# Paired row statistics, roots on ScalarE, the hidden layer computed ahead, and the dense rows' mean taken off on VectorE

## The chip, the cores and the metric

The kernel is one program on one core of a Trainium2 chip. The metric is the device time in microseconds (us), the median over several executions. All data is fp32, and the whole layer is one launch.

## The reference, cut to what matters

A graph network layer over N = 100,000 nodes with 160 features and 25,000 edges, sorted by their destination. It has two halves, and each begins with a layer norm and a ReLU of the node rows. Only the parts that the change touches are spelled out.

```python
def _layernorm(x, axis=-1, eps=1e-05):
    m = jnp.mean(x, axis=axis, keepdims=True)
    v = jnp.var(x, axis=axis, keepdims=True)
    return (x - m) / jnp.sqrt(v + eps)

h = jnp.maximum(_layernorm(x, axis=-1), 0.0)
x = x + _L0_gnn_ref(h, node_vec1, edge_attr_4, edge_attr_8, ...)   # sc(h), lin1(h)[src], edge net, lin2, cos and sin of an angle
h = jnp.maximum(_layernorm(x, axis=-1), 0.0)
x = x + _L1_gnn_ref(h, edge_attr_4, ...)                           # message of h[src], segment_sum, relu
# inside _L0_gnn_ref, for every edge:
h = jax.nn.silu(edge_scalars @ fc_w1 * (1.0 / np.sqrt(8.0)))
weight = h @ fc_w2 * (1.0 / np.sqrt(64.0))
```

Because the deviation is positive, relu((x - m) / s) is relu(x - m) / s. The kernel uses this in the first half: only the mean is taken off before the matrix products, and 1/s is multiplied in afterwards, together with `node_vec1`.

## The kernel before, in words

The kernel runs in a start and three phases, with five engines that each follow their own written list of steps; semaphores join them. In the tables below a stage ends where the next one's first work begins.

**The start** builds index tables from the sorted edges, stores them to DRAM with SyncE's queue (lines 410 to 419), multiplies weights together and scales them. SyncE waits for the stores (`s_tab_out`) and then loads the first edge quad.

**Phase 1** goes over 98 dense units `u` of 1024 nodes (128 partitions x `GD` = 8 rows; `U` = 98) and at the same time over 196 edge tiles of 128 edges. Four tiles make a quad `q` (`GQ` = 4; `Q` = 49), so a quad goes with two units. For a unit, VectorE takes `bn_stats` of each of the 8 rows (`dense_stats`, line 1334), and three parts of small instructions turn the two half-row moments that `bn_stats` leaves into minus mean and variance (`moment_part`, lines 1203 to 1210; `rest_of`, line 1215, takes the mean off the first 32 columns). ScalarE takes the mean off the other 128 columns with the ReLU in the same instruction (`dense_relu`, line 763, 8 instructions), TensorE transposes the rows (`dense_tr`, line 964), ScalarE copies them from PSUM (`dense_copy`, line 770), TensorE multiplies (`linear`, lines 969 and 970), VectorE adds the result times a scale to x (`dense_x1`, line 1353) and takes the statistics of the new rows (`dense_stats2`, line 1362, and again `moment_part`). GpSimd raises the variance to the power -0.5 (`inverse_root`, line 628), forms the scale and the shift (lines 635 and 642), ScalarE writes the normed rows (`dense_h1`, line 755), and GpSimd adds them to x (`dense_y`, line 625). Two DMAs store both.

For an edge quad GpSimd gathers the source rows (`p1_gather`, line 581, four indirect DMAs), the same statistics, moments, ReLU (line 782) and transposes follow; TensorE's `net_mm` and ScalarE's `net_silu` (lines 1025 and 775) compute the hidden layer of the quad; then each tile goes through `p1_source`, the features on VectorE (lines 1421, 1426, 1430), `p1_feat_t` (line 1083), `p1_parts`, the message (lines 1402, 1409) and `p1_sum` (line 1069). Each engine's order inside a unit is written in its `step(u)`, which has two halves, `slot(u, 0)` and `slot(u, 1)`. TensorE's `dense_tr` waits until ScalarE has copied the sum of `p1_sum` out of the same PSUM bank (`e_tot`, line 810).

**Phase 2** goes over the 49 quads again. GpSimd gathers the destination rows (`p2_gather`, four indirect DMAs at line 581) and later scatters the new h rows (`p2_scatter`, four at line 587). Between them lie on VectorE the statistics (line 1528), moments, eight small angle steps (`p2_angle`, lines 1543 to 1560), scales, the sums at lines 1589 and 1599, the second statistics (line 1608) and moments. Here the root is already ScalarE's (`p2_root1`, `p2_root2`, lines 896 and 901), and each quad switches ScalarE's function table to the sine and back.

**Phase 3** computes the second half's messages over the 196 tiles; the change does not touch it.

Of the kernel before, what the change touches and what calls it, by code (L numbers as in the profile page):

```python
# [19 lines left out]
P = 128  # L20
GD = 8
# [53 lines left out]
def gnn_kernel(nc, xa, src, dst, number, edges_in, scalars_in, scalars_t_in, wpack, out):  # L75
# [19 lines left out]
    sum_tab = scratch("sum_tab", (Q, P, GQ * CW))  # L95
    y_tab = scratch("y_tab", (Q, P, GQ * D))
# [23 lines left out]
    with ExitStack() as ctx:  # L120
# [34 lines left out]
        minus_half = sb("minus_half", [P, GD])  # L155
# [21 lines left out]
        st1, st2 = four("st1", [P, GD, 6]), two("st2", [P, GD, 6])  # L177
        su1, su2 = four("su1", [P, GD, 2]), two("su2", [P, GD, 2])
        df1, df2 = four("df1", [P, GD]), two("df2", [P, GD])
        sq1, sq2 = four("sq1", [P, GD]), two("sq2", [P, GD])  # L180
        m21, m22 = four("m21", [P, GD]), two("m22", [P, GD])
        neg1, neg2 = four("neg1", [P, GD]), two("neg2", [P, GD])
        var1, var2 = four("var1", [P, GD]), two("var2", [P, GD])
# [16 lines left out]
        q_sct = two("q_sct", [GQ * SW, P])  # L200
# [5 lines left out]
        hr_e = two("hr_e", [P, GQ * 32])  # L206
# [9 lines left out]

        x_q = [x_all[:, i * GQ * XW:(i + 1) * GQ * XW] for i in range(4)]
# [4 lines left out]
        st_e = two("st_e", [P, GQ, 6])  # L222
        su_e = two("su_e", [P, GQ, 2])
        df_e = two("df_e", [P, GQ])
        sq_e = two("sq_e", [P, GQ])
        m2_e = two("m2_e", [P, GQ])
        neg_e = two("neg_e", [P, GQ])
        var_e = two("var_e", [P, GQ])
        sd_e = two("sd_e", [P, GQ])
        sd2 = two("sd2", [P, GQ])  # L230
# [38 lines left out]
        n_act = sem("net_hidden_ready")  # L269

        d_in = [sem(f"x_loaded{i}") for i in range(4)]
        d_ln1 = sem("dense_moments1")
        d_relu = sem("dense_h_ready")
# [6 lines left out]
        d_ln2 = sem("dense_moments2")  # L280
        d_h1 = sem("dense_h1_ready")
# [5 lines left out]
        e_tb = sem2("p1_tables_loaded")  # L287
        e_scl = sem("p1_scale_ready")
        e_g = sem2("p1_source_rows")
        e_ln = sem("p1_moments")  # L290
        e_relu = sem("p1_h_ready")
# [27 lines left out]
        r_relu = sem("p2_h_ready")  # L319
# [31 lines left out]
        def x3(t, w, g):  # L351
            return t[:, :].rearrange("p (g f) -> p g f", g=g, f=w)

# [14 lines left out]
        def _(sp):  # L368
# [53 lines left out]
            sp.wait_ge(s_rows, 32)  # L422
            sp.wait_ge(s_tab_out, 16 * n_out)
# [16 lines left out]
            def p1_load(q):  # L440
                j = q.mod(2)
                wait(sp, e_g[j], q.over(2, 64))
                sp.dma_start(i_src[j][:, :], src_tab[q.times(1)]).then_inc(e_ix[j], 16)
                wait(sp, n_mm, q.times(1, -1))
                sp.dma_start(q_sct[j][:, :], scalars_t[q.times(1)]).then_inc(n_in[j], 16)
# [121 lines left out]
        def _(pool):  # L567
            nc.gpsimd.memset(t_next[:, :], N + 5).then_inc(s_fill, 1)
            nc.gpsimd.memset(t_prev[:, :], -1).then_inc(s_fill, 1)
            nc.gpsimd.memset(minus_half[:, :], -0.5)  # L570
# [40 lines left out]
            def p1_gather(q):  # L611
                j = q.mod(2)
                pool.wait_ge(e_ix[j], q.over(2, 16, 16))
                wait(pool, e_relu, q.times(1, -1))
                wait(pool, e_scl, q.times(2, -2))
                gather(xa, x_e[j], XW, i_src[j], e_g[j])
# [10 lines left out]
            def inverse_root(inv, var, n, signal):  # L627
                nc.gpsimd.tensor_tensor(inv[:, 0:n], var[:, 0:n], minus_half[:, 0:n], ALU.pow).then_inc(signal, 1)  # L628

            def dense_scale(u):  # L630
                j = u.mod(4)
                pool.wait_ge(d_ln1, u.times(5, 4))
                inverse_root(inv1[j], var1[j], GD, d_scl)
                pool.wait_ge(d_scl, u.times(2, 1))
                nc.gpsimd.tensor_tensor(scl1[j][:, :], inv1[j][:, :], x3(x_in[j], XW, GD)[:, :, D], ALU.mult).then_inc(d_scl, 1)

            def dense_norm2(u):
                j = u.mod(2)
                pool.wait_ge(d_ln2, u.times(4, 4))
                inverse_root(inv2[j], var2[j], GD, d_nmr)  # L640
                pool.wait_ge(d_nmr, u.times(2, 1))
                nc.gpsimd.tensor_tensor(nmr2[j][:, :], neg2[j][:, :], inv2[j][:, :], ALU.mult).then_inc(d_nmr, 1)  # L642
# [9 lines left out]
            def step(w):  # L652
                q = At(w.i, w.c // 2, 2)
                if w.mod(2) == 1 and (q + 1).within(Q):
                    p1_gather(q + 1)
                if (w - 1).within(U):
                    dense_scale(w - 1)
                if (w - 4).within(U):
                    dense_y(w - 4)
                if (w - 3).within(U):  # L660
                    dense_norm2(w - 3)
                if w.mod(2) == 0 and q.within(Q):
                    p1_scale(q)
# [3 lines left out]
            for w in range(8):  # L667
                step(At(0, w))
            with pool.Fori(2, U // 4) as i:
                for c in range(4):  # L670
                    step(At(i, c))
            for w in range(U - 2, U + 4):
# [74 lines left out]
        def _(act):  # L747
# [11 lines left out]
            def dense_relu(u, h):  # L759
                act.wait_ge(d_ln1, u.times(5, 3))  # L760
                x, hh = x_in[u.mod(4)], hb[u.mod(2)]
# [1080 lines left out]
```

## Time and profile before

| what | value |
|---|---|
| time, median of 3 runs | 2476.07 us (2475.62 to 2479.8) |
| profiled execution, first to last instruction | 2863.6 us |
| instructions | 55863 |
| busy share of the span: PE, PEld, DVE, ACT, POOL | 68%, 64%, 68%, 54%, 61% |
| mean granted TensorE clock | 0.828 of full |
| HBM traffic | 130 GB/s over the span |

The profiled execution's own time is given only as its span, 2863.6 us; nothing around the span is on the page. It is 387.5 us more than the median of the runs. PE is TensorE's matmul, PEld its weight load, DVE is VectorE, ACT is ScalarE, POOL is GpSimd and SPq SyncE's queue. A busy share is an average over the phases.

### The profile page before, as it was taken

The numbers are of one execution on the slowest core, as the hardware profiler recorded it, in microseconds if no ns is written. First come the engines' busy times: TensorE is split into PE (matmuls) and PEld (weight loads), VectorE is DVE, ScalarE is ACT, GpSimd is POOL, SyncE is SP. The second block draws the span as 40 slices with busy tenths as digits, with TensorE's granted clock in tenths as the row PEclk, the third lists the DMA queues.
The fourth block names the chain that finished last, engine by engine and source line by source line (L and its number), as shares of the span: only waits on it lengthen the run. The fifth ranks groups of instructions, "written<-read, shape, count | busy, mean of one in ns | idle before, by whom it ended". The sixth has DMA issues, their size and how long they took to land.

```text
span 2863.6 us, 55863 instructions
## 1 busy us (share of the span) xinstructions
PE 1940.9 (68%) x12874; PEld 1820.7 (64%) x12874; DVE 1954.7 (68%) x8628; ACT 1560.1 (54%) x4412; POOL 1745.2 (61%) x1676
## 2 busy tenths in 40 slices
PE   0888888878878888878883343434344777777877
PEld 0777777777877777777773333323233777767777
DVE  2889888887888888888884655556555444444444
ACT  0667677776777777777774444545453222222222
POOL 1656666665666666766656565655565666666665
PEclk9989999998999999999995555555555999999898
DMA  9444544443444444454543232323332333333332
GB/s 79 142 143 169 172 170 171 172 172 138 169 172 170 173 169 164 162 179 147 180 154 124 87 89 87 93 87 97 88 99 83 81 89 88 92 92 90 94 95 74
DMA packets 223602, 364.52 MB, mean 127 GB/s; under 512 B 115938, under 2 KB 133149, under 8 KB 223405
## 3 DMA queue, kind: packets, MB, share of 16 engines
q1 hardware_dynamic: 176524, 289.81, 32.1%
q0 software_dynamic: 47040, 74.31, 9.8%
q14 instruction: 27, 0.21, 0.0%
q8 instruction: 11, 0.18, 0.0%
HBM read 176.85 MB, written 194.78 MB: 130 GB/s over the span
## 4 chain that ended last, share of the span: by engine, by line
DVE 31%; PE 25%; issue 14%; another core or an unknown queue 11%; POOL 8%; ACT 6%; SPq 2%; DMA 1%; DVEq 1%; ACTq 0%; POOLq 0%
DVE st L1334 3%; PE bank L969 3%; PE bank L1154 3%; POOL x_e L581 3%; POOL inv L628 3%; DVE x L1353 2%; DVE su_e L1203 2%; PE bank L964 2%; PE bank L1166 2%; DVE st L1362 2%; PE bank L1163 2%; ACT h L755 2%; PE bank L1176 2%; DVE x L1599 2%
## 5 line engine op out<-in xcount | busy, mean ns | idle before, releaser
L628 POOL TENSOR_TENSOR inv<-var,minus_half 128x8 f32<-128x8 f32 x196 | 327.7, 1672 | 256.5 <-DVE var L1210 253.4
L625 POOL TENSOR_TENSOR yo<-x,h 128x640 f32<-128x640 f32 x196 | 305.8, 1560 | 147.8 <-ACT h L755 145.4
L969 PE MATMUL bank<-wp,hT 128*128 128x160 f32 x1568 | 392.6, 334 | 1.6 <-DVE x L1353 0.7
L755 ACT ACTIVATE h<-x,nmr,inv 128x160 f32<-128x160 f32 x784 | 342.2, 514 | 6.1 <-POOL nmr L642 6.1
L587 POOL DMA_INDIRECT h_all<-h,i_put x196 | 203.4, 1038 | 217.9 <-ACT h L871 146.0
L964 PE MATMUL bank<-ident,h_e 128*128 128x128 f32 x392 | 83.0, 350 | 358.9 <-ACT h_e L878 229.2
L587 POOL DMA_INDIRECT out<-yo,i_put x196 | 202.1, 1031 | 197.2 <-DVE feat L1706 63.8
L1353 DVE SCALAR_TENSOR_TENSOR x<-bank,scl,x_all 128x160 f32<-128x160 f32 x784 | 254.3, 372 | 89.1 <-PE bank L970 46.0
L969 PE MATMUL bank<-wp,eT 128*128 128x160 f32 x784 | 274.5, 444 | 54.5 <-ACT eR L886 27.3
L934 ACT ACTIVATE tot<-bank 128x160 f32<-128x160 f32 x196 | 59.6, 304 | 455.7 <-remote 207.1
L964 PEld LDWEIGHTS bank<-ident,h_e 128*128 128x128 f32 x392 | 57.5, 184 | 367.9 <-DVE hr_e L1215 244.1
L1715 DVE TENSOR_TENSOR xr<-bank,q_ed 128x96 f32<-128x96 f32 x196 | 50.0, 255 | 334.0 <-PE bank L1166 175.6
L970 PEld LDWEIGHTS bank<-wp,hR 128*128 128x128 f32 x1568 | 268.4, 199 | 0.0
L970 PE MATMUL bank<-wp,hR 128*128 128x64 f32 x1568 | 268.4, 254 | 0.0
L581 POOL DMA_INDIRECT x_e<-in_xa,i_src x192 | 192.0, 1000 | 109.5 <-issue 48.0
L969 PEld LDWEIGHTS bank<-wp,hT 128*128 128x128 f32 x1568 | 253.0, 202 | 3.1 <-DVE x L1353 0.9
L763 ACT ACTIVATE hb<-x_all,neg 128x128 f32<-128x128 f32 x784 | 248.7, 394 | 0.0
L719 POOL DMA_INDIRECT h<-h_all,i_src x196 | 202.3, 1032 | 61.9 <-issue 58.4
L581 POOL DMA_INDIRECT x_all<-in_xa,i_dst x196 | 194.5, 992 | 65.6 <-issue 58.4
L1154 PE MATMUL bank<-ident,feat 128*128 128x128 f32 x784 | 136.1, 301 | 136.2 <-DVE feat L1706 109.8
L969 PEld LDWEIGHTS bank<-wp,eT 128*128 128x128 f32 x784 | 171.3, 270 | 73.8 <-issue 46.5
L964 PE MATMUL bank<-ident,hb 128*128 128x128 f32 x784 | 131.7, 294 | 117.7 <-ACT tot L810 115.9
(173 smaller groups left out, 6292.4 us busy)
## 6 DMA issues: line engine op xcount, KB each, us to landing
x_all<-in_xa SPq DMA_DIRECT2D x98, 644.0 KB, 5.8
h_all<-h SPq DMA_DIRECT2D x98, 640.0 KB, 2.9
out<-yo SPq DMA_DIRECT2D x98, 640.0 KB, 3.3
q_row<-row_tab SPq DMA_DIRECT2D x98, 256.0 KB
sum_tab<-tot SPq DMA_DIRECT2D x49, 322.0 KB, 4.2
y_tab<-yo SPq DMA_DIRECT2D x49, 320.0 KB
x<-y_tab SPq DMA_DIRECT2D x49, 320.0 KB
cv<-sum_tab SPq DMA_DIRECT2D x25, 322.0 KB
```

Of the source, the lines that this page charges most:

```text
L581: nc.gpsimd.indirect_dma_start(into[:, t * width:(t + 1) * width], None, rows, bass.IndirectOffsetOnAxis(ap=index[:, t:t + 1], axis=0)).th ...
L587: nc.gpsimd.indirect_dma_start(rows, bass.IndirectOffsetOnAxis(ap=index[:, t:t + 1], axis=0), tile, None, bounds_check=N - 1, oob_is_err=F ...
L625: nc.gpsimd.tensor_tensor(yo[j][:, a:b], x1[j][:, a:b], h1[j][:, a:b], ALU.add).then_inc(d_y, 1)
L628: nc.gpsimd.tensor_tensor(inv[:, 0:n], var[:, 0:n], minus_half[:, 0:n], ALU.pow).then_inc(signal, 1)
L719: nc.gpsimd.indirect_dma_start(h1[j][:, t * D:(t + 1) * D], None, h1_all, bass.IndirectOffsetOnAxis(ap=i_src[j][:, t:t + 1], axis=0)).then ...
L755: ins = nc.scalar.activation(h1[j][:, k * D:(k + 1) * D], x1[j][:, k * D:(k + 1) * D], ACT.Relu, bias=nmr2[j][:, k:k + 1], scale=inv2[j][: ...
L763: ins = nc.scalar.activation(hh[:, k * P:(k + 1) * P], x[:, k * XW + 32:k * XW + D], ACT.Relu, bias=neg1[u.mod(4)][:, k:k + 1])
L964: nc.tensor.transpose(ps_main[:, t * P:(t + 1) * P], main[:, t * P:(t + 1) * P], ident[:, :])
L969: nc.tensor.matmul(dst_ps, main[:, t * P:(t + 1) * P], wp[:, w:w + D], start=True, stop=False)
L970: return nc.tensor.matmul(dst_ps[:, 0:DS], rest[:, :], wp[:, w + D + t * DS:w + D + (t + 1) * DS], start=False, stop=True)
L1154: ins = nc.tensor.transpose(bank[n.mod(2)][:, c * P:(c + 1) * P], feat[n.mod(2)][:, c * P:(c + 1) * P], ident[:, :])
L1353: ins = V.scalar_tensor_tensor(x1[j][:, k * D:(k + 1) * D], bank[2 + pair % 2][:, k % 2 * D:(k % 2 + 1) * D], scl1[u.mod(4)][:, k:k + 1], ...
```

## The change

It has seven parts.

1. **Statistics of two rows at once.** `paired_stats` reads two rows interleaved, element by element, with one `bn_stats`; the two half moments that it leaves are then those of the two rows. `moment_part` and `rest_of` go, with their buffers and semaphore steps.
2. **Mean off ahead of the transposes, ReLU behind them.** For the dense rows VectorE does it with two instructions (`dense_centre`), for phase 2 as well (`p2_centre`), for phase 1's edge rows GpSimd (`p1_centre`). `dense_relu`, `p1_relu` and `p2_relu` on ScalarE go; the copies out of PSUM become ReLUs.
3. **Roots.** ScalarE takes `Sqrt` of the dense variances (`dense_root1`, `dense_root2`), VectorE the reciprocal, the scale and the shift. GpSimd keeps the power -0.5 for the edge rows alone (`p1_scale`).
4. **SiLU stage.** The edge net's hidden layer is computed for all quads before phase 1, 4 quads to a group, 13 groups, stored to `hid_tab` in DRAM and loaded quad by quad in phase 1.
5. **GpSimd's order.** The gather stands at the even step, `dense_y` follows with a lag of 3 and not 4, and `p1_centre` and `p1_scale` stand at the odd step.
6. VectorE's order of the small steps in `step(u)` and `p2_step(q)` follows from this.
7. `hr_e` becomes one buffer, and `x1` and `yo` serve as the buffers of the SiLU stage.

```diff
+            def net_load(g):
+                n = min(GQ, Q - g * GQ)
+                wait(sp, n_mm, 2 * (g - 1))
+                sp.dma_start(n_sct[g % 2][:, 0:n * P].rearrange("f (q p) -> f q p", p=P),
+                             scalars_t[g * GQ:g * GQ + n].rearrange("q f p -> f q p")).then_inc(n_in[g % 2], 16)
+
+            def net_store(g):
+                n = min(GQ, Q - g * GQ)
+                sp.wait_ge(n_act, 2 * g + 2)
+                sp.dma_start(hid_tab[g * GQ:g * GQ + n].rearrange("q p f -> p q f"),
+                             n_hid[g % 2][:, 0:n * 2 * P].rearrange("p (q f) -> p q f", f=2 * P)).then_inc(n_st[g % 2], 16)
+
+            net_load(0)
+            for g in range(NB):
+                if g + 1 < NB:
+                    net_load(g + 1)
+                net_store(g)
+            for j in range(2):
+                sp.wait_ge(n_st[j], 16 * ((NB + 1 - j) // 2))
...
+            def centre(into, rest, rows, st, g, signal):
+                x = x3(rows, XW, g)
+                nc.gpsimd.tensor_tensor(x3(into, P, g), x[:, :, 32:D], bc_last(stat(st, g, 1), P), ALU.subtract)
+                nc.gpsimd.tensor_tensor(x3(rest, 32, g), x[:, :, 0:32], bc_last(stat(st, g, 1), 32),
+                                        ALU.subtract).then_inc(signal, 1)
...
             def p1_scale(q):
                 j = q.mod(2)
-                pool.wait_ge(e_ln, q.times(5, 4))
-                inverse_root(inv_e[j], var_e[j], GQ, e_scl)
-                pool.wait_ge(e_scl, q.times(2, 1))
+                nc.gpsimd.tensor_scalar(sd_e[j][:, :], stat(st_e[j], GQ, 2), 1.0 / D, EPS, ALU.mult, ALU.add).then_inc(e_scl, 1)
+                pool.wait_ge(e_scl, q.times(3, 1))
+                nc.gpsimd.tensor_tensor(inv_e[j][:, :], sd_e[j][:, :], minus_half[:, :], ALU.pow).then_inc(e_scl, 1)
+                wait(pool, e_gg, q.times(GQ, -GQ))
+                pool.wait_ge(e_scl, q.times(3, 2))
...
+            def root(into, st, n, signal):
+                nc.scalar.activation(into[:, 0:n], stat(st, n, 2), ACT.Sqrt, bias=eps[:, :],
+                                     scale=1.0 / D).then_inc(signal, 1)
...
-                nc.scalar.activation(hT[h][:, :], bank[0][:, :], ACT.Copy)
+                nc.scalar.activation(hT[h][:, :], bank[0][:, :], ACT.Relu)
...
+            def paired_stats(st, pair, rows, width):
+
+                two_rows = rows[:, 2 * pair * width:(2 * pair + 2) * width].rearrange("p (g f) -> p f g", f=width)
+                return V.bn_stats(st[:, 2 * pair:2 * pair + 2, :].rearrange("p g k -> p (g k)"), two_rows[:, 0:D, :])
...
             def dense_stats(u):
                 j = u.mod(4)
                 v.wait_ge(d_in[j], u.over(4, 16, 16))
-                for k in range(GD):
-                    ins = V.bn_stats(st1[j][:, k, :], x_in[j][:, k * XW:k * XW + D])
+                for pair in range(GD // 2):
+                    ins = paired_stats(st1[j], pair, x_in[j], XW)
                 ins.then_inc(d_ln1, 1)
 
-            def dense_moments(u, part):
+            def dense_centre(u):
+                j, x = u.mod(2), x3(x_in[u.mod(4)], XW, GD)
+                v.wait_ge(d_ln1, u.times(1, 1))
+                wait(v, d_tr, u.times(2, -2))
+                V.tensor_tensor(x3(hb[j], P, GD), x[:, :, 32:D], bc_last(stat(st1[u.mod(4)], GD, 1), P), ALU.subtract)
+                V.tensor_tensor(x3(hr[j], 32, GD), x[:, :, 0:32], bc_last(stat(st1[u.mod(4)], GD, 1), 32),
+                                ALU.subtract).then_inc(d_cen, 1)
+
+            def dense_inverse(u):
                 j = u.mod(4)
-                v.wait_ge(d_ln1, u.times(5, part))
-                moment_part(part, st1[j], su1[j], df1[j], sq1[j], m21[j], neg1[j], var1[j], GD, d_ln1)
+                v.wait_ge(d_sq1, u.times(1, 1))
+                V.reciprocal(inv1[j][:, :], sd1[j][:, :]).then_inc(d_scl, 1)
...
             dense_stats(At(0, 0))
-            for part in (1, 2, 3):
-                dense_moments(At(0, 0), part)
-            dense_rest(At(0, 0))
+            dense_centre(At(0, 0))
             p1_stats(At(0, 0, 2))
-            for part in (1, 2, 3):
-                p1_moments(At(0, 0, 2), part)
-            p1_rest_rows(At(0, 0, 2))
             p1_selectors(At(0, 0, 2))
+            for j in range(2):
+                v.wait_ge(n_st[j], 16 * ((-(-Q // GQ) + 1 - j) // 2))
```

## Rows read from the trace of the kernel before

**Rows 1.** Busy time in phases 1, 2, 3: from:to, length, PE, PEld, DVE, ACT, POOL, clock

```profile
66.00:1490.00 1424.00, 1155.24 (x8202) 1088.07 (x8203) 1214.51 (x5175) 1026.71 (x3051) 923.39 (x866) 0.93 0.47 164
1490.00:2190.00 700.00, 273.55 (x1111) 245.25 (x1109) 409.80 (x2300) 348.25 (x773) 408.01 (x400) 0.53 0.31 94
2190.00:2863.60 673.60, 508.66 (x3528) 485.38 (x3528) 315.22 (x1078) 183.83 (x588) 407.21 (x395) 0.90 0.34 88
```

**Rows 2.** Waits in 400 to 1300 us: total us, times, longest

```profile
PE bank L964 <- ACT tot L810: 76.1, 93, 1.9
PE bank L1083 <- DVE feat L1430: 52.4, 32, 3.0
PE bank L1083 <- ACT eR L790: 23.8, 14, 2.8
```

**Rows 3.** Groups by form in 400 to 1300 us: count | busy us, mean ns | idle before

```profile
L1203 DVE TENSOR_TENSOR su_e<-st_e 128x8 f32<-128x8 f32 x31 | 40.5, 1306 | 0.0
L1210 DVE TENSOR_TENSOR var<-m,sq 128x8 f32<-128x8 f32 x123 | 40.4, 328 | 0.0
L1207 DVE SCALAR_TENSOR_TENSOR sq_e<-df_e 128x4 f32<-128x4 f32 x31 | 4.6, 149 | 0.0
L763 ACT ACTIVATE hb<-x_all,neg 128x128 f32<-128x128 f32 x492 | 156.1, 393 | 0.0
L628 POOL TENSOR_TENSOR inv<-var,minus_half 128x8 f32<-128x8 f32 x123 | 205.0, 1667 | 158.2 <-DVE var L1210 156.1
L625 POOL TENSOR_TENSOR yo<-x,h 128x640 f32<-128x640 f32 x123 | 192.2, 1563 | 81.5 <-ACT h L755 79.7
```

**Rows 4.** VectorE's instructions in time, phase 1: start us, us

```profile
742.22 0.68 DVE L1374 TENSOR_TENSOR same<-q_row,q_key 128x512 f32<-128x512 f32 x1
742.82 0.68 DVE L1374 TENSOR_TENSOR carry<-q_row,q_key 128x512 f32<-128x512 f32 x1
...
748.44 1.91 DVE L1334 BATCH_NORM_STATS2 st<-x_all 128x6 f32<-128x160 f32 x8
...
750.84 0.17 DVE L1203 TENSOR_TENSOR su<-st 128x16 f32<-128x16 f32 x1
750.92 0.17 DVE L1204 TENSOR_TENSOR df<-st 128x8 f32<-128x8 f32 x1
...
754.67 1.31 DVE L1203 TENSOR_TENSOR su_e<-st_e 128x8 f32<-128x8 f32 x1
```

**Rows 5.** GpSimd's instruction in time that those meet

```profile
754.41 1.54 POOL L625 TENSOR_TENSOR yo<-x,h 128x640 f32<-128x640 f32 x1
```

**Rows 6.** From the start into phase 1, instructions in time

```profile
62.53 0.38 SPq L419 DMA_DIRECT2D row_tab<-t_row  x1
65.63 0.37 SPq L443 DMA_DIRECT2D i_src<-src_tab  x1
...
69.62 0.38 ACT L775 ACTIVATE q_hid<-bank 128x256 f32<-128x256 f32 x1 [67.59 <-PE bank L1025]
```

**Rows 7.** Groups of the whole trace, and a DMA issue (KB each, us to landing)

```profile
L770 ACT ACTIVATE hT<-bank 128x512 f32<-128x512 f32 x196 | 117.0, 597 | 135.1 <-PE bank L965 133.5 <-issue 1.6
...
L1025 PE MATMUL bank<-q_sct,wp 32*128 32x128 f32 x196 | 35.6, 302 | 49.3 <-DMA q_sct<-scalars_t 49.3
...
h_all<-h SPq DMA_DIRECT2D x98, 640.0 KB, 2.9
```

**Rows 8.** GpSimd's instructions in time, phase 2

```profile
1752.61 1.02 POOL L587 DMA_INDIRECT h_all<-h,i_put  x1 [0.30 <-issue]
...
1762.90 1.02 POOL L587 DMA_INDIRECT h_all<-h,i_put  x1 [0.30 <-issue]
...
1783.43 1.02 POOL L587 DMA_INDIRECT h_all<-h,i_put  x1 [10.55 <-ACT h L871]
```

**Rows 9.** Groups by form in 1490 to 2190 us: idle before a removed instruction

```profile
L1206 DVE TENSOR_SCALAR neg<-su 128x4 f32<-128x4 f32 x49 | 9.0, 183 | 38.4 <-remote 30.5 <-issue 6.7
...
L1206 DVE TENSOR_SCALAR neg_e<-su_e 128x4 f32<-128x4 f32 x49 | 8.5, 174 | 7.7 <-remote 6.5 <-DVE df_e L1204 1.0 <-issue 0.2
```

More of the change, by code:

```diff
@@ L613, in p1_gather @@
                 pool.wait_ge(e_ix[j], q.over(2, 16, 16))
-                wait(pool, e_relu, q.times(1, -1))
-                wait(pool, e_scl, q.times(2, -2))
+                wait(pool, e_cen, q.times(1, -1))
                 gather(xa, x_e[j], XW, i_src[j], e_g[j])
@@ L653, in step @@
                 q = At(w.i, w.c // 2, 2)
+                if w.mod(2) == 0 and (q + 1).within(Q):
+                    p1_gather(q + 1)
+                if (w - 3).within(U):
+                    dense_y(w - 3)
                 if w.mod(2) == 1 and (q + 1).within(Q):
[L655 to L663, printed above, removed]
+                    p1_centre(q + 1)
+                    p1_scale(q + 1)
             pool.wait_ge(s_tab_in, 80)
             gather(xa, x_e[0], XW, t_src, e_g[0])
-            for w in range(8):
+            p1_centre(At(0, 0, 2))
+            p1_scale(At(0, 0, 2))
+            for w in range(4):
                 step(At(0, w))
-            with pool.Fori(2, U // 4) as i:
+            with pool.Fori(1, U // 4) as i:
                 for c in range(4):
                     step(At(i, c))
-            for w in range(U - 2, U + 4):
+            for w in range(U - 2, U + 3):
                 step(At(0, w))
@@ L851, in step @@
                     dense_h1(u - 2, 1)
-            net_silu(At(0, 0, 2))
-            p1_relu(At(0, 0, 2))
+            for g in range(-(-Q // GQ)):
+                net_silu(g)
             p1_copy(At(0, 0, 2))
@@ L1093, in slot @@
                 if (s - 1).within(T):
-                    p1_feat_t(s - 1, q1 if u.mod(2) == 0 and h == 1 and q1.within(Q) else None)
+                    p1_feat_t(s - 1)
                 if (s - 2).within(T):
@@ L1102, in step @@
             def step(u):
-                q = At(u.i, u.c // 2, 2)
-                odd = u.mod(2) == 1
                 slot(u, 0)
-                if not odd and (q + 1).within(Q):
-                    net_mm(q + 1)
                 if u.within(U):
@@ L1114, in _ @@
             pe.wait_ge(e_z, 1)
-            net_mm(At(0, 0, 2))
+            for g in range(-(-Q // GQ)):
+                net_mm(g)
+            pe.wait_ge(n_act, 2 * -(-Q // GQ))
             p1_tr(At(0, 0, 2))
@@ L1379, in p1_stats @@
                 v.wait_ge(e_g[j], q.over(2, 64, 64))
-                for t in range(GQ):
-                    ins = V.bn_stats(st_e[j][:, t, :], x_e[j][:, t * XW:t * XW + D])
+                for pair in range(GQ // 2):
+                    ins = paired_stats(st_e[j], pair, x_e[j], XW)
                 ins.then_inc(e_ln, 1)
-            def p1_moments(q, part):
-                j = q.mod(2)
-                v.wait_ge(e_ln, q.times(5, part))
-                moment_part(part, st_e[j], su_e[j], df_e[j], sq_e[j], m2_e[j], neg_e[j], var_e[j], GQ, e_ln)
-            def p1_rest_rows(q):
-                rest_of(hr_e[q.mod(2)], x_e[q.mod(2)], neg_e[q.mod(2)], GQ, e_ln)
             def p1_selectors(q):
@@ L1439, in step @@
                 rows = u.mod(2) == 0 and q1.within(Q)
+                odd = u.mod(2) == 1 and q1.within(Q)
                 if now:
                     dense_x1(u - 1, 0)
+                if (u - 2).within(U):
+                    dense_inverse2(u - 2)
+                if now:
                     dense_x1(u - 1, 1)
+                if (u - 2).within(U):
+                    dense_shift2(u - 2)
+                if now:
                     dense_stats2(u - 1, 0)
@@ L1606, in p2_stats2 @@
                 v.wait_ge(r_x1, q.times(2, 2))
-                for t in range(GQ):
-                    ins = V.bn_stats(st2[j][:, t, :], x1[j][:, t * D:(t + 1) * D])
+                for pair in range(GQ // 2):
+                    ins = paired_stats(st2[j], pair, x1[j], D)
                 ins.then_inc(r_ln2, 1)
-            def p2_moments2(q, part):
-                j = q.mod(2)
-                v.wait_ge(r_ln2, q.times(4, part))
-                moment_part(part, st2[j], su2[j], df2[j], sq2[j], m22[j], neg2[j], var2[j], GQ, r_ln2)
             def p2_norm2(q, part):
@@ L1674, in p2_step @@
                     p2_angle(q, 7)
-                if b:
-                    for part in (1, 2, 3):
-                        p2_moments2(q - 1, part)
             v.wait_ge(d_y, 2 * U)
```

257 lines of the change are left out of this document (104 added, 153 removed).

## The prediction

> **What bounds the kernel now.** I read the stages first, then the waits of a steady stretch, then the groups by form, then single instructions in time. Phase 1 takes 1424 us, phase 2 700 us and phase 3 673.6 us [rows 1]; the start before them takes 66 us. Phase 1 is 98 units long, so a unit takes 1424 / 98 = 14.53 us. In it VectorE is busy 1214.51 / 98 = 12.39 us, TensorE 11.79, ScalarE 10.48 and GpSimd 9.42 [rows 1]. No engine is full. VectorE is nearest, and TensorE is close behind. The reader should see two things in TensorE's waits. One is the wait for the copy of the sum, which the change leaves: 76.1 us in 900, which hold 61.9 units, so 1.23 us a unit. The other is the wait for features and for ScalarE's edge copy: 52.4 + 23.8 us, again 1.23 us a unit [rows 2]. It comes from VectorE and ScalarE being late, and the change can shorten it.
>
> Phase 2 has 49 quads of 14.29 us. TensorE runs at about half clock there and has 273.55 us of work in 700; it bounds nothing [rows 1]. GpSimd issues eight indirect DMAs for a quad. In a burst this takes 1762.90 - 1752.61 = 10.29 us; after three quads it stands still, here for 10.55 us, until ScalarE's h is there [rows 8]. So phase 2 swings between GpSimd's floor of 10.3 us and a chain through VectorE.
>
> **The start.** SyncE has issued the last table store at 62.53 and goes on at 65.63, and the first SiLU is at 69.62 [rows 6]. The new stage can begin at 62.9. It has 13 groups. Each needs a load, two products of 512 columns, two SiLUs of 512 columns and a store of 512 KB. A ScalarE copy of 512 columns takes 0.60 us, and a store of 640 KB lands after 2.9 us [rows 7], so I take 1.2 us for both SiLUs and 2.5 to 2.9 us for the store. The product of a 128-column piece takes 0.30 us in its records [rows 7], two records to a piece. At that rate 512 columns would take up to 2.4 us; pipelined I take 0.9. Two buffers let two groups overlap. The store is followed by the SiLU of the group after next, so two groups take 0.5 + 2.9 + 1.2 = 4.6 us at least, and with the load in the loop (about 2 us, as the table load before phase 1 [rows 6]) 5 us. That is 2.5 us a group, 32 us for 13, and 3 us for the last landing. Against it stand the 3 us of table stores that it covers. **Start: +32 us**, from +20 (if only the SiLUs and issues counted) to +50 (products at 2.4 us each). Nothing hides it: TensorE and VectorE both wait for its end.
>
> **VectorE in phase 1.** A small instruction takes 0.08 us from start to start when it isn't held up, one of 512 elements 0.60 us, so an element costs 1.03 ns; eight row statistics take 1.91 us, the ends overlapping, so 0.23 us each [rows 4].
> - Removed, moments: 12 instructions a unit and 6 a quad, 15 a unit. Their twelve groups run from 40.5 us down to 4.6 [rows 3] and sum to 233 us, or 3.8 a unit. Unimpeded they would overlap to 15 x 0.08 = 1.2 us. They hold 930 instructions; the surplus over an undisturbed record of 0.165 us each (153 us) is 80 us, or 1.3 a unit: instructions held up, as the one of 1.31 us which usually takes 0.17 [rows 4]. Together -2.5 us.
> - Removed, statistics: a pair costs 0.23 + 160 x 1.03 ns = 0.39 us in place of 0.46. Nine pairs a unit give -0.6. The interleaved read isn't in the trace; I take its element at the same price, and bound it by twice that, +2.4 a unit. Edge rest rows: -0.1.
> - Added: the centring of 1024 elements, 0.60 + 512 x 1.03 ns = 1.13 us (the 256-element one exists already), and four small ones, 0.3 us.
> - Sum: -1.8 us; VectorE is busy 10.6 us a unit.
>
> **The other engines in phase 1.** ScalarE loses 8 ReLUs of 0.393 us a unit and 4 a quad of the same size: -3.9 us, against two roots of about 0.2 each. GpSimd loses two powers of 1.67 us [rows 3] and two small ones, and gains the edge centring: at the add's 1.56 us for 640 elements [rows 3], 640 elements a quad are 1.56, 0.8 a unit. It comes to about 6.6 us. TensorE loses only the edge net, 35.6 / 98 = 0.36 us a unit [rows 7], and keeps 11.4.
>
> **Phase 1, sum.** VectorE with 10.6 no longer bounds. TensorE has 11.4 + 1.23 = 12.7 us, and of the other 1.23 us wait I keep half, because features still go TensorE, ScalarE, VectorE, TensorE in every tile, and VectorE's second half of a unit got the long centring. That is 13.3 us: 98 x -1.2 = **-118 us**. The ends are -180 (12.7 a unit) and -35 (only the edge net's time). GpSimd's new steps have slack: the gather starts after the last source product of the quad before, needs 4 x 1.3 us [rows 8] and a landing, and VectorE wants its rows some 10 us into the unit. Where this cover is gone, VectorE's statistics would stand behind it with the features queued after them.
>
> **Phase 2.** VectorE loses 12 small instructions (-0.96 us) and 4 x 0.07 us of statistics, and gains a centring of 512 elements (+0.6). ScalarE loses four ReLUs in the chain from row to product, 1.6 us. More is in the idle time ahead of the removed instructions: six groups wait between 38.4 and 7.7 us [rows 9], 147 us together, 3.0 us a quad, and this falls in the burst. A part will move to the angle steps, which stand behind the same DMAs. I take half of the 3.0 and 0.6 of work: -2.0 a quad, **-98 us**. The ends are 0 and -4.0 (GpSimd's floor). Phase 3 doesn't change.
>
> **Sum.** +32 - 118 - 98 = -184 us, 6.4% of the profiled 2863.6 us. The median of the runs is 387.5 us below that span, and no row says which phase has this surplus. Scaled by 0.935 the median becomes 2316 us. If the stalls of phase 2 are mostly the surplus, the gain there is smaller; I forecast **2320 us**.
>
> **Rivals.**
> - *TensorE holds.* Of the products nothing goes but 0.36 us a unit, and both its waits stay because they are the latency of a loop between engines. Phase 1 gives 0.36 to 0.75 us a unit, at most 35 to 74 us and say 55, phase 2 nothing because GpSimd's floor of 10.3 us may already hold in the timed runs, and the start costs 32: -23, scaled by 0.865 -20, some 2456 us. For it: the busy numbers of TensorE and VectorE are only 0.6 apart [rows 1]. Against: waits for late features are in the rows [rows 2].
> - *The centring is held up.* An instruction of VectorE with two inputs in SBUF ran 1.31 us in place of 0.17, from 754.67 to 755.98, while GpSimd's add ran from 754.41 to 755.95 [rows 4, 5]. If each centring waits out one add of 1.56 us and the features after it wait too, VectorE's saving of 1.8 falls to 0.2, and if GpSimd's new edge centring then meets the transposes it loses 0.8 more: phase 1 +59 us. With the start +32 and phase 2 at 0 this is +91, or 2555 us scaled. It decides from the point where VectorE's held-up time grows by over 1.8 us a unit. Against: the removed instructions are fifteen chances a unit to be held up, the new ones six, and GpSimd is busy 3 us less.
> - *The stalls go altogether.* Phase 1 at 12.7 us and phase 2 at 10.3: -180 - 196 + 32 = -344 us, times 0.865 gives 2180 us.
>
> The page "SBUF — State Buffer" of the Trainium skill, section "Who interferes with whom", states for the second rival that a VectorE instruction with two SBUF inputs and a GpSimd instruction that reads SBUF exclude each other for the whole instruction, whichever came first going first. The trace agrees, with the 1.31 us above. By that rule the new edge centring on GpSimd can be held up too, by VectorE's 1.13 us centring, and this speaks against the change.
>
> **How the numbers follow.** Forecast case (2250 to 2400): 0.57. TensorE holds: 0.20. Held up: 0.08. All stalls go: 0.15. About 0.2% is what a measurement here can tell from no change. TensorE-holds puts 0.04 within it and the rest of its share on faster, so faster 0.88, same 0.04, slower 0.08. The range 2190 to 2460 leaves out the held-up case, an end of each of the other two, 0.18 in all.
>
> **What would show it.** Start: the first feature instruction some 32 us later. Phase 1: a unit of about 13.3 us, VectorE at 10.6, ScalarE at 7.0, GpSimd at 6.6; TensorE's wait for features halved and its wait for the sum's copy as before. A paired statistic with a record of about 0.47 us; at 0.7 or more the interleaved read is dear. A 1024-element centring at about 1.2 us; a mean over 2 us is the second rival. Phase 2: about 12.3 us a quad, GpSimd's standstills shorter. The forecast is wrong if a unit of phase 1 stays above 14 us or falls below 12.7, or if the start adds more than 50 us.

## The result: 11.6% slower, and the profile after

The changed kernel takes 2768.2 us (median of 4 runs, 2756.0 to 2769.8) against 2477.9 us for the kernel before on the same chip: a ratio of 1.116, 95% interval 1.114 to 1.119. The forecast was 2320 us. It was wrong in sign.

The trace of before in the rows above was of a slower execution (span 2863.6 us) than any timed run. The same kernel, traced again unchanged (label `before_again`), spans 2471.2 us, and everything below is compared with that trace. I cut the stages by the first and last start of one instruction each: ScalarE's copy of the source product (`g_e`) for phase 1, VectorE's first angle step for phase 2 and its first feature instruction for phase 3.

| stage | before, traced again | after | difference |
|---|---|---|---|
| first source copy | 70.2 us | 116.6 us | +46.4 |
| phase 1, first to last source copy | 1321.5 | 1556.4 | +234.9 |
| phase 2 | 484.1 | 494.7 | +10.6 |
| phase 3 | 517.3 | 522.2 | +4.9 |

Windows by stage (from:to, length, busy PE, PEld, DVE, ACT, POOL, granted clock, DMA share, GB/s), first of before traced again, then of after; they answer to [rows 1].

```profile
70.20:1391.70 1321.50, 1105.44 (x8201) 1041.79 (x8202) 1197.07 (x5178) 1023.04 (x3047) 905.75 (x863) 0.97 0.50 176
1420.70:1904.80 484.10, 258.23 (x1008) 231.11 (x1008) 371.95 (x2182) 321.86 (x712) 368.16 (x368) 0.54 0.39 119
```

```profile
116.60:1673.00 1556.40, 1160.94 (x8008) 1093.51 (x8008) 1064.67 (x3297) 794.98 (x2220) 655.59 (x622) 0.89 0.44 154
1700.80:2195.50 494.70, 256.01 (x1008) 228.85 (x1008) 342.40 (x1469) 278.54 (x519) 381.43 (x367) 0.53 0.40 116
```

VectorE, ScalarE and GpSimd all do less work in phase 1 than before, as they were to, and yet a unit takes 1556.4 / 97.5 = 15.96 us in place of 13.55 (the first and the last of 196 copies lie 195 tiles, or 97.5 units, apart). So something is waited for. The waits of after in 400 to 1300 us, which answer to [rows 2] (total us, times, longest; a choice of them), name it; the last line is SyncE's queue's own.

```profile
DVE same L1380 <- DMA q_row<-row_tab: 256.6, 28, 9.7
PE bank L977 <- DVE x L1354: 140.6, 28, 5.5
ACT h L770 <- DVE nmr L1207: 137.9, 28, 5.4
...
SPq L465 <- PE bank L1062: 641.6, 28, 24.1
```

These 900 us hold 28 quads. Once in each, VectorE stands still for 9.2 us until the row of destinations (`q_row`) has landed, and TensorE and ScalarE wait behind it. SyncE has been standing for 22.9 us of the quad's 32 at line 465, which is `q_hid`, waiting for the source product of line 1062. In this part the diff has a hunk. My sections above name the load in it, but neither they nor the prediction speak of its wait. It stands in `p1_load(q)`:

```diff
                 j = q.mod(2)
                 wait(sp, e_g[j], q.over(2, 64))
                 sp.dma_start(i_src[j][:, :], src_tab[q.times(1)]).then_inc(e_ix[j], 16)
-                wait(sp, n_mm, q.times(1, -1))
-                sp.dma_start(q_sct[j][:, :], scalars_t[q.times(1)]).then_inc(n_in[j], 16)
+                wait(sp, e_pw, q.times(GQ, -GQ))
+                sp.dma_start(q_hid[j][:, :], hid_tab[q.times(1)]).then_inc(e_hid[j], 16)
```

`p1_load(q + 1)` stands in SyncE's even step and `p1_tables(q)`, which loads `q_key`, `q_ed` and `q_row`, in the odd step behind it. The buffer of `q_hid` comes free only with the last source product of the quad that used it before. In time, the queue and then VectorE:

```profile
713.59 0.33 SPq L465 DMA_DIRECT2D q_hid<-hid_tab  x1
714.19 0.36 SPq L456 DMA_DIRECT2D h_all<-h  x1
714.64 0.38 SPq L458 DMA_DIRECT2D out<-yo  x1
715.22 0.71 SPq L448 DMA_DIRECT2D x_all<-in_xa  x1
716.12 1.25 SPq L470 DMA_DIRECT2D q_key<-key_tab  x1
717.55 0.55 SPq L471 DMA_DIRECT2D q_ed<-edges  x1
718.19 0.45 SPq L472 DMA_DIRECT2D q_row<-row_tab  x1
```

```profile
714.64 0.25 DVE L1428 TENSOR_TENSOR feat<-feat,q_ed 128x96 f32<-128x96 f32 x1
724.40 0.69 DVE L1380 TENSOR_TENSOR same<-q_row,q_key 128x512 f32<-128x512 f32 x1 [9.51 <-DMA q_row<-row_tab]
```

The release at 713.6 lets seven DMAs go one after the other. `q_row` is the last, 4.6 us later, and it lands 6.2 us after that. VectorE has wanted it since 714.9. A load that nobody needs soon holds back one that is needed in the same step.

### The profile page after: what moved, and what is told of

It is laid out like the page before. It is cut to its first block, busy times and chain, and to the rows that moved or that the text cites. A ratio compares the mean times of both kernels' runs of the same rounds, so it can differ in the third digit from the quotient of the medians.

```text
span 2765.6 us, 51473 instructions
## 1 busy us (share of the span) xinstructions
PE 1942.8 (70%) x12730; PEld 1808.3 (65%) x12730; DVE 1764.9 (64%) x5982; ACT 1298.2 (47%) x3409; POOL 1487.9 (54%) x1432
## 4 chain that ended last, share of the span: by engine, by line
PE 33%; DMA 19%; issue 15%; SPq 10%; DVE 9%; ACT 7%; POOL 6%; DVEq 1%; POOLq 0%; ACTq 0%
DMA q_row<-row_tab 13%; PE bank L977 8%; PE bank L978 4%; ACT h L770 3%; DMA x_all<-in_xa,i_dst 3%; POOL h_all L608 3%; PE bank L1086 2%; PE bank L972 2%; SPq L470 2%; PE bank L1062 2%; POOL x_all L602 2%; DMA out<-yo,i_put 2%; DVE x L1354 2%; PE bank L1154 2%; PE bank L1049 2%
## 5 line engine op out<-in xcount | busy, mean ns | idle before, releaser
L977 PE MATMUL bank<-wp,hT 128*128 128x160 f32 x1568 | 447.7, 372 | 232.3 <-DVE x L1354 231.4
L977 PEld LDWEIGHTS bank<-wp,hT 128*128 128x128 f32 x1568 | 280.9, 224 | 246.4 <-DVE x L1354 242.4
L1380 DVE TENSOR_TENSOR same<-q_row,q_key 128x512 f32<-128x512 f32 x98 | 67.8, 692 | 582.3 <-DMA q_row<-row_tab 582.2
L602 POOL DMA_INDIRECT x_e<-in_xa,i_src x192 | 225.6, 1175 | 159.9 <-issue 85.0
L978 PEld LDWEIGHTS bank<-wp,hR 128*128 128x128 f32 x1568 | 306.8, 225 | 0.0
L978 PE MATMUL bank<-wp,hR 128*128 128x64 f32 x1568 | 295.4, 275 | 0.0
L1354 DVE SCALAR_TENSOR_TENSOR x<-bank,scl,x_all 128x160 f32<-128x160 f32 x784 | 253.8, 365 | 10.6 <-PE bank L978 10.1
L608 POOL DMA_INDIRECT h_all<-h,i_put x196 | 214.7, 1095 | 61.7 <-issue 59.1
L1203 DVE BATCH_NORM_STATS2 st<-x 128x6 f32<-128x320 f32 x490 | 218.0, 485 | 0.0
L791 ACT ACTIVATE hT<-bank 128x512 f32<-128x512 f32 x196 | 117.0, 597 | 208.4 <-PE bank L973 208.4
L972 PE MATMUL bank<-ident,hb 128*128 128x128 f32 x784 | 124.7, 282 | 110.0 <-ACT tot L828 104.1
L978 PEld LDWEIGHTS bank<-wp,eR 128*128 128x128 f32 x784 | 183.7, 265 | 0.0
```

The lines of the kernel that those rows point to most:

```text
L602: nc.gpsimd.indirect_dma_start(into[:, t * width:(t + 1) * width], None, rows, bass.IndirectOffsetOnAxis(ap=index[:, t:t + 1], axis=0)).th ...
L608: nc.gpsimd.indirect_dma_start(rows, bass.IndirectOffsetOnAxis(ap=index[:, t:t + 1], axis=0), tile, None, bounds_check=N - 1, oob_is_err=F ...
L791: nc.scalar.activation(hT[h][:, :], bank[0][:, :], ACT.Relu)
L972: nc.tensor.transpose(ps_main[:, t * P:(t + 1) * P], main[:, t * P:(t + 1) * P], ident[:, :])
L977: nc.tensor.matmul(dst_ps, main[:, t * P:(t + 1) * P], wp[:, w:w + D], start=True, stop=False)
L978: return nc.tensor.matmul(dst_ps[:, 0:DS], rest[:, :], wp[:, w + D + t * DS:w + D + (t + 1) * DS], start=False, stop=True)
```

## The experiments

The theory from here on (A): the new wait at the head of an in-order queue is the whole loss, by what stands behind it. Its rival (B): the new work itself is dear, in the centring on VectorE, the statistics or GpSimd's steps, and the wait for `q_row` only shows where slack collects.

### The kernel before, traced again

> The kernel before, unchanged, for a second trace. Theory A (the first trace of the kernel before was of a disturbed execution): span near 2476 us, phase 3 near the 550 us that the changed kernel's trace shows for the same code, phase 2 near 510 us, phase 1 near 1340 us (13.7 us a unit). Theory B (the profile itself costs 387 us): span near 2860 us again.

One run of 2473.0 us, span 2471.2. Phase 1 takes 13.55 us a unit, phase 2 10.09 us a quad, phase 3 517 us. Cut in the same way, the trace above has 14.53, 13.5 and 645, so its surplus lay in all three. Its stalls of phase 2 are not there again: GpSimd's wait for ScalarE's h, as in [rows 8], is 3.8 us in the whole phase ahead of the scatters, where the first trace has 146.0, and the idle time ahead of `neg` in [rows 9] is 1.7 us in place of 38.4. So nearly half of my forecast gain (98 of 216 us) had little under it.

### The wait put into the kernel before

```diff
                 sp.dma_start(q_key[j][:, :], key_tab[q.times(1)]).then_inc(e_tb[j], 16)
+                wait(sp, e_pw, q.times(GQ))
                 sp.dma_start(q_ed[j][:, :], ed_q[q.times(1)]).then_inc(e_tb[j], 16)
```

> The kernel before with one more wait on SyncE's queue: ahead of the load of the edge attributes, for the last source product of the quad before. Queue theory (a wait on SyncE's queue for that product makes the quad's tables late): slower by 150 to 300 us, VectorE waits for q_row at the selectors by 3 to 8 us a quad. Rival (the work moved onto VectorE and the new order cost the time): within 20 us of the kernel before.

2627.2 us, ratio 1.062 (1.056 to 1.067). With nothing of the change but this wait, 149 us are lost, and the waits are of the same kind:

```profile
DVE same L1375 <- DMA q_row<-row_tab: 44.8, 29, 2.0
PE bank L1084 <- DVE feat L1431: 107.3, 48, 3.8
...
SPq L452 <- PE bank L1058: 301.1, 29, 12.7
```

It is released at the same product as in the changed kernel, but only two short DMAs follow, so VectorE waits 1.5 us a quad for `q_row` and not 9; I had expected 3 to 8. The loss is still half of that of the change. VectorE's features come behind the selectors (`same` and `carry`, which need `q_row`), and TensorE's wait for them is 107.3 us where it was 57.7. How the loss divides between this and the other DMAs that stand behind the wait is not separated.

### The same wait, two tiles earlier

```diff
+                wait(sp, e_pw, q.times(GQ, -2))
```

> As the kernel before with the added wait, but for the product two tiles earlier (the third last and not the last of the quad before), one dense unit sooner. Queue theory: what counts is how late the tables come, so most of the 149 us goes; 0 to 50 us above the kernel before. If instead a wait on TensorE's product is dear in itself: still above 100 us.

2478.45 us, ratio 0.9997 (0.9983 to 1.0011). In its trace SyncE never stands at this wait between 400 and 1300 us: the product is always done when SyncE comes to it. So the instruction as such costs nothing, and the 149 us come from the standing. That standing too can be free is shown further below, where SyncE stands 5.0 us a quad and nobody waits for what is behind.

### The load of the hidden layer on ScalarE's queue

```diff
-                wait(sp, e_pw, q.times(GQ, -GQ))
-                sp.dma_start(q_hid[j][:, :], hid_tab[q.times(1)]).then_inc(e_hid[j], 16)
...
+                if not odd and (q + 1).within(Q):
+                    wait(act, e_pw, q.times(GQ))
+                    nc.scalar.dma_start(q_hid[(q + 1).mod(2)][:, :], hid_tab[(q + 1).times(1)]) \
+                        .then_inc(e_hid[(q + 1).mod(2)], 16)
```

> The changed kernel with the hidden layer's load of a quad issued from ScalarE, right behind the copy that waits for the same product, so that SyncE's queue has no such wait. Queue theory: 2768 falls by 9.5 us a quad less ScalarE's issue time, to 2250 to 2400 us, and VectorE's wait for q_row is gone. Rival: above 2650 us.

2454.6 us, ratio 0.990 (0.987 to 0.992): 11.6% slower has become 1.0% faster by moving one load of 128 KB. The rest of the change is unaltered, the 128 KB are still moved, and the loss is gone. Theory B is out as its cause.

### The load kept on SyncE, behind the tables

```diff
                 if v.mod(2) == 1 and q.within(Q):
                     p1_tables(q)
+                if v.mod(2) == 1 and (q + 1).within(Q):
+                    p1_hidden(q + 1)
```

> The changed kernel with only the order on SyncE's queue changed: the hidden layer's load of quad q+1, with its wait, stands behind the tables of quad q and no longer a unit ahead of them. Queue theory: as the load from ScalarE within 2%, 2250 to 2420 us. Rival: above 2650 us.

2452.4 us, ratio 0.991 (0.988 to 0.993), the same as on the other queue within the spread of the runs. SyncE still waits for that product, 5.0 us a quad, and no one waits for SyncE. Phase 1 from 115.8 to 1354.8, 12.71 us a unit; the clock in 400 to 1300 us is 1.00 where it was 0.88. This is the change as it was meant, and the rest of the runs start from it. Its window in 400 to 1300 us, SyncE's wait and VectorE groups there:

```profile
400.00:1300.00 900.00, 754.45 (x5820) 709.68 (x5818) 854.20 (x2404) 580.27 (x1624) 473.02 (x461) 1.00 0.56 196
```

```profile
SPq L468 <- PE bank L1068: 176.4, 35, 5.1
```

```profile
L1209 DVE BATCH_NORM_STATS2 st<-x 128x6 f32<-128x320 f32 x284 | 126.0, 483 | 0.0
...
L1338 DVE TENSOR_TENSOR hb<-x_all,st 128x1024 f32<-128x1024 f32 x71 | 86.2, 1214 | 0.0
L1434 DVE TENSOR_TENSOR feat<-feat,q_ed 128x96 f32<-128x96 f32 x141 | 79.6, 564 | 0.0
...
L1350 DVE TENSOR_TENSOR scl<-inv,x_all 128x8 f32<-128x8 f32 x71 | 46.1, 649 | 0.0
...
L1213 DVE SCALAR_TENSOR_TENSOR nmr<-st,inv 128x8 f32<-128x8 f32 x71 | 28.6, 403 | 0.0
```

The paired statistic (0.48 us) and the centring (1.21 us) have the length that was forecast. But VectorE is busy 854.2 of 900 us, 12.05 us a unit and not 10.6. Three instructions are too long: the last feature product (line 1434), the scale (line 1350) and the shift (line 1213). In the changed kernel, where the engines meet less, the first two took 247 and 160 ns. In time they look so, VectorE first, then GpSimd:

```profile
705.26 1.14 DVE L1350 TENSOR_TENSOR scl<-inv,x_all 128x8 f32<-128x8 f32 x1
...
721.38 2.08 DVE L1434 TENSOR_TENSOR feat<-feat,q_ed 128x96 f32<-128x96 f32 x1
```

```profile
704.83 1.54 POOL L651 TENSOR_TENSOR yo<-x,h 128x640 f32<-128x640 f32 x1 [4.24 <-ACT h L776]
...
721.78 1.55 POOL L651 TENSOR_TENSOR yo<-x,h 128x640 f32<-128x640 f32 x1
```

Each ends within 0.15 us of the end of GpSimd's add (706.40 and 706.37; 723.46 and 723.33); the second begins 0.40 us ahead of the add's record and still ends with it. The same end is found for every long one in the 900 us: for the 34 of 141 last feature products that take over 0.5 us, for 36 of 71 scales and for 35 of 71 shifts.

### GpSimd's long add made short

```diff
                     a, b = h * GQ * D, (h + 1) * GQ * D
+                    b = a + 8
                     nc.gpsimd.tensor_tensor(yo[j][:, a:b], x1[j][:, a:b], h1[j][:, a:b], ALU.add).then_inc(d_y, 1)
```

> As the kernel with the table loads ahead of the hidden-layer load (2452.4 us), but GpSimd's two adds of a unit in phase 1, h + x of 640 elements and 1.55 us each, add only the first 8 elements of each 640; the rest of the first output's dense part stays zero, so that part of the computation is left out. Theory: three two-input instructions of VectorE (the last feature product 0.564 us in the mean, the scale 0.649, the shift 0.403) are long because they begin during such an add and end with it; without the long add they should have means near 0.25, 0.16 and 0.16 us. That takes 2 x 0.31 + 0.49 + 0.24 = 1.35 us a unit off VectorE's 12.05 and leaves 10.7, close to the 10.6 that was predicted. With VectorE 95% busy in a unit of 12.71 us the unit falls towards TensorE's floor, some 11.9 to 12.3 us, and the time to 2375 to 2415 us. Rival: the three are long for another reason (their place in the order, the tile they read); then their means stay over 0.4 us and the time falls by under 10 us.

The kernel leaves out 632 of every 640 elements of the sum h + x. It takes 2405.0 us, ratio 0.966 (0.965 to 0.968), where the kernel it starts from has 0.991; its span is 44.5 us below. The kernel before took 2487.3 us beside it, more than in the other comparisons, so the ratio says more than the microseconds. The three groups, and the window:

```profile
L1438 DVE TENSOR_TENSOR feat<-feat,q_ed 128x96 f32<-128x96 f32 x147 | 36.6, 249 | 0.0
...
L1217 DVE SCALAR_TENSOR_TENSOR nmr<-st,inv 128x8 f32<-128x8 f32 x73 | 19.8, 272 | 0.0
...
L1354 DVE TENSOR_TENSOR scl<-inv,x_all 128x8 f32<-128x8 f32 x74 | 12.0, 162 | 0.0
```

```profile
400.00:1300.00 900.00, 779.19 (x6075) 737.96 (x6075) 797.01 (x2503) 596.78 (x1694) 313.52 (x471) 1.00 0.59 204
```

The last feature product fell from 564 to 249 ns and the scale from 649 to 162; the shift only to 272 (0.16 expected). The other half of it is held up by another instruction of GpSimd, the subtraction of the edge rows' mean: 36 of the 73 shifts take 0.39 us, and each of them ends within 0.03 us of it.

```profile
715.13 0.39 DVE L1217 SCALAR_TENSOR_TENSOR nmr<-st,inv 128x8 f32<-128x8 f32 x1
```

```profile
714.46 1.05 POOL L656 TENSOR_TENSOR h_e<-x_e,st_e 128x512 f32<-128x512 f32 x1
```

VectorE is at 797.01 / 73.75 units = 10.8 us, the forecast's 10.6 nearly. The unit gained 0.5 us (12.20) for 1.25 us of VectorE's work. That GpSimd's add held these instructions up is shown.

### Each paired statistic as two single ones

```diff
-                return V.bn_stats(st[:, 2 * pair:2 * pair + 2, :].rearrange("p g k -> p (g k)"), two_rows[:, 0:D, :])
+                V.bn_stats(st[:, 2 * pair:2 * pair + 2, :].rearrange("p g k -> p (g k)"), rows[:, 2 * pair * width:2 * pair * width + D])
+                a = st.shape[1] // 2 + 2 * pair
+                b = (2 * pair + 1) * width
+                return V.bn_stats(st[:, a:a + 2, :].rearrange("p g k -> p (g k)"), rows[:, b:b + D])
```

> The kernel with the tables first, and every paired statistic replaced by two instructions of one row each (the second one's result isn't used, so the norm is taken from half rows of one row: the output differs). 9 more instructions a unit at 0.06 us each. If VectorE bounds phase 1: slower by 40 to 60 us than 2452. If not: within 15 us.

2596.5 us, ratio 1.048 (1.045 to 1.051): 144 us, 1.46 us a unit in phase 1 (14.17), from an addition of about 0.54 us a unit to VectorE. I had expected 40 to 60 us.

```profile
400.00:1300.00 900.00, 723.25 (x5182) 681.70 (x5182) 784.86 (x2708) 516.58 (x1445) 410.94 (x412) 0.93 0.50 175
```

VectorE had been busy 95% of the time; now it is 87%, so the unit grew by waiting and not by VectorE's own length. TensorE's wait for features rose from 30 to 74 us and its granted clock fell from 1.00 to 0.93; its own busy time rose from 10.7 to 11.4 us a unit, about half of the 1.46. How the rest divides between late features and held-up instructions isn't separated. In this one case an addition cost nearly three times its own length.

### The dense centring on GpSimd

GpSimd does it at the head of its step:

```diff
+                if w.within(U):
+                    dense_centre(w)
                 if w.mod(2) == 0 and (q + 1).within(Q):
                     p1_gather(q + 1)
...
-                if ahead:
-                    dense_centre(u + 1)
```

> The kernel with the tables first, and the dense rows centred on GpSimd (at the head of its step) instead of VectorE. VectorE loses 1.63 us of 12.0 a unit, GpSimd gains some 2.6 us. If VectorE bounds phase 1 now (busy 95%): faster by 50 to 120 us than 2452. If TensorE and the loops between the engines bound it: 2430 to 2475. If GpSimd's reads hold VectorE's two-input instructions up as much again, or the transposes wait for GpSimd: slower, 2480 to 2600.

2423.6 us, ratio 0.977 (0.975 to 0.980). A unit takes 12.37 us, 0.34 less for 1.6 us off VectorE. These 29 us lie between the ranges that I had given for a phase bound by VectorE (50 to 120 us) and for one that is not (at most 22). VectorE is now busy 83% of the time, and it waits for GpSimd's add to be done with the buffer of x1, 104.1 us where the kernel before, traced again, has 29.9:

```profile
DVE x L1367 <- POOL yo L651: 104.1, 36, 3.2
```

### The SiLU stage's DMAs on ScalarE's queue

Loads, SiLUs and stores are all issued by ScalarE, beside SyncE's table stores:

```diff
+            act.wait_ge(n_go, 1)
+            net_load(0)
+            for g in range(NB):
+                if g + 1 < NB:
+                    net_load(g + 1)
                 net_silu(g)
+                net_store(g)
```

> The kernel with the tables first, and the SiLU stage's loads and stores issued from ScalarE's queue as soon as the scalars are in DRAM, beside the 40 us in which SyncE issues the table stores. The stage is 13 groups of 3.9 us, bound by TensorE's 512-column products. If it then runs from 27 to some 77 us: phase 1 starts at 80 and not at 115, 2452 falls by 30 to 38 us to about 2417. If the two queues' descriptors hold each other up: less than 10 us.

2439.2 us, ratio 0.984 (0.982 to 0.987). The stage begins at 27 us and not at 62, but ends at about 92 and not at 110, so 13 us are gained and not the 30 to 38 expected. TensorE waited up to 11.7 us for a load, while SyncE's stores of the index tables ran beside it; that they are the reason was not tried:

```profile
42.30 10.82 SPq L415 DMA_DIRECT2D key_tab<-f_key  x1
45.44 3.78 PE L1042 MATMUL bank<-yo,wp 32*128 32x512 f32 x4 [11.68 <-DMA yo<-scalars_t]
```

### All three together

> The hidden-layer load behind the table loads, the dense centring on GpSimd, and the SiLU stage's DMAs issued from ScalarE's queue, all three together. If the three gains are of different places (queue order in phase 1, VectorE's work in phase 1, the start) they add: the kernel with the first two took 2423.6 us, and the third was worth 13 us on the first alone (2452.4 to 2439.2), so 2410 us, phase 1 at 12.4 us a unit as with the first two, and the first source copy at about 98 us in place of 116. Rival: with SyncE held until the stage's stores have landed only later, part of the start's gain comes back as a later first unit, or the gain in phase 1 of the second depended on the first tiles being late; then over 2420 us.

2405.85 us, ratio 0.970 (0.968 to 0.971): the fastest kernel that computes everything. Phase 1 goes from 102.8 to 1308.5, 12.37 us a unit. The gains add up: the ratios of the two single edits, 0.977 and 0.984 / 0.991, multiply to 0.97. The first source copy comes at 102.8 us and not at 98.

## Why the prediction was wrong

**The step that failed** is the sum of phase 1, -118 us: it counts the four computing engines and no cost for SyncE's queue. The load of `q_sct`, free early, was replaced by the load of `q_hid`, free late, and I never asked what was queued behind the new wait. It is worth 2768.2 - 2452.4 = 316 us, shown in three ways: by the other queue (-314), by order alone (-316), and by such a wait put into the kernel before (+149, and 0 when released two tiles earlier). None of my rivals had it; my slower case was another mechanism. The change with its queue mended gives -25 us, where I forecast -156. Its 2452.4 us lie at the 2456 of my first rival (TensorE holds), but in part by luck: the start cost 46 us and not 32, phase 1 gave 82.5 and not 55, and phase 2 lost 12 where the rival had nothing.

**Start, +32 (20 to 50): mis-sized.** Measured +46. A group takes 3.9 us; I had 2.5. My product of 512 columns at 0.9 us was most of the error: a SiLU of 0.60 us follows the one before after 1.71 us, waiting for TensorE.

```profile
61.80 7.16 PE L1033 MATMUL bank<-yo,wp 32*128 32x512 f32 x8 [42.70 <-DMA yo<-scalars_t]
...
65.58 0.60 ACT L799 ACTIVATE x<-bank 128x512 f32<-128x512 f32 x1 [1.11 <-PE bank L1033]
```

The bound of 2.4 from the rows was nearer than the value I took for pipelining.

**VectorE in phase 1, -1.8 us a unit.** The terms that rest on lengths held: a paired statistic 0.40 us from start to start (1.70 us for four; 0.39 forecast), its interleaved read at no extra price, the centring 1.21 us. The term that failed is the 1.3 us of held-up time taken as removed with the instructions that showed it. With the queue mended VectorE had 12.05 us a unit, and some 1.4 us of long times stood on three other instructions. (In the kernel as given it had 1064.67 / 98 = 10.9 us; the engines meet less there.) The cause was GpSimd's add, which the change leaves; [rows 4] and [rows 5] showed it, and I used it for a rival on the centring only. That rival was wrong in its place: the centring is not held up (1.21 us). Other two-input instructions are.

**The other engines.** GpSimd 655.59 / 98 = 6.7 us a unit (6.6 forecast). ScalarE 794.98 / 98 = 8.1, not 7.0. I took ten ReLUs a unit at a record's length, 0.393 us, but [rows 3] say 156.1 us for 492, so 0.32 us each, since the records overlap; that is 0.8 us, and the two roots took 0.29 us each and not 0.2. Against this stands the SiLU that left phase 1 and that I did not count, 12.7 us in 900 or 0.2 a unit, so about 0.3 us a unit stay without an account.

**Phase 1, -118 (-180 to -35).** In the kernel as given +235. With the queue mended -82.5, inside the ends; 12.71 us a unit against 13.3, but from a before of 13.55 and not 14.53, so 0.84 us a unit gained and not 1.2. Where they come from, by the window and TensorE's waits in 400 to 1300 us, first before traced again, then with the tables first (its window stands above):

```profile
400.00:1300.00 900.00, 751.28 (x5577) 707.84 (x5577) 814.44 (x3530) 697.96 (x2077) 623.44 (x594) 0.97 0.51 179
```

```profile
PE bank L964 <- ACT tot L810: 58.9, 99, 0.6
PE bank L1083 <- DVE feat L1430: 57.7, 33, 2.6
PE bank L1083 <- ACT eR L790: 32.5, 33, 1.0
```

```profile
PE bank L978 <- ACT tot L834: 80.1, 141, 0.6
PE bank L1092 <- ACT eR L814: 34.6, 35, 1.0
PE bank L1092 <- DVE feat L1434: 30.4, 36, 0.9
```

TensorE's busy time fell by 0.65 us a unit, where I had 0.36 for the edge net; the granted clock rose from 0.97 to 1.00. Its wait for features and for the edge copy fell by 0.44 us (1.36 to 0.92), a third and not the half that I kept. Its wait for the sum's copy, which I left as it was, grew by 0.24. And VectorE, which was no longer to bound the unit, stayed the busiest engine at 95%.

**Phase 2, -98 (-196 to 0).** Measured +10.6. GpSimd's floor held already, as the first rival said: 10.09 us a quad, with hardly a wait of GpSimd for another engine. It got a little worse, by its own scatters (before traced again, then after, both in phase 2):

```profile
L587 POOL DMA_INDIRECT h_all<-h,i_put x179 | 182.5, 1019 | 58.1 <-issue 54.3 <-ACT h L871 3.8
```

```profile
L608 POOL DMA_INDIRECT h_all<-h,i_put x179 | 198.0, 1106 | 55.9 <-issue 54.0 <-ACT h L885 1.9
```

In the stretch that I read, one of four scatter issues takes 1.4 to 1.5 us in place of 1.0, while VectorE runs its new centring and its add without a gap:

```profile
1914.66 0.68 DVE L1522 TENSOR_TENSOR h_e<-x_all,st_e 128x512 f32<-128x512 f32 x1
1915.26 0.28 DVE L1523 TENSOR_TENSOR hr_e<-x_all,st_e 128x128 f32<-128x128 f32 x1
...
1915.54 0.82 DVE L1614 TENSOR_TENSOR yo<-x,h 128x640 f32<-128x640 f32 x1
```

```profile
1913.52 1.00 POOL L608 DMA_INDIRECT h_all<-h,i_put  x1 [0.30 <-issue]
1914.83 1.37 POOL L608 DMA_INDIRECT h_all<-h,i_put  x1 [0.30 <-issue]
```

The scatters' 15.5 us more are enough for the whole of the 10.6. That VectorE's instructions are the reason is read from the traces and was not tried; in before traced again the add alone, 0.81 us long, ran beside an issue of 0.99 us.

**The sizing basis.** I saw that the trace was 387.5 us over the runs and that no row said where, and scaled all stages by one factor. The surplus was largest in phase 2 (3.4 us of 13.5 a quad), where I drew 98 us from it.

On holding up, the page "SBUF — State Buffer" of the Trainium skill, section "Who interferes with whom", states that a VectorE instruction with two inputs in SBUF contends with a GpSimd instruction that reads SBUF, and that the pair of ports they share is an exclusive lock. The short-add run agrees: 564 to 249 ns.

## What to carry to other kernels

When a load gets a new buffer and so a new release, find its queue and read what is issued behind it and when that is wanted; a load that waits long belongs behind the urgent ones, or on a queue where none stand behind it. Held-up time belongs to the engine that holds, not to the instruction that shows it: here it went when the add was made short, and had only moved when the instructions that showed it were removed. And when the profiled span is far above the timed runs, the waits in it are no basis for a gain until a second trace shows them too.

## What the runs showed of the hardware

- One `bn_stats` over two interleaved rows of 160 took 0.48 us (0.40 from start to start), two single ones 0.31 us each (0.23), so 0.46 for both: reading with a stride of 640 bytes or more showed no cost.
- A subtraction with two inputs in SBUF of 1024 elements took 1.21 us on VectorE and 1.91 us on GpSimd.
- With the SiLU stage on ScalarE's queue, each of four DMAs in a row that store the index tables held SyncE for 8.9 to 13.0 us; three of them write pieces of 16 or 32 bytes. The first store of that kind, ahead of them, took 0.42 us. Beside them TensorE waited up to 11.7 us for a load from ScalarE's queue.
- An fp32 product of 512 columns with a depth of 32 took 1.7 us, in two instructions 0.86 us apart.
- In the 900 us read, every VectorE instruction of the three held-up groups that was long ended within 0.15 us of the end of GpSimd's add.
